# DLRM tower with a compressed interaction network: the first MLP layer in high and low halves, and the third cross layer's halves divided anew

## What is computed

```python
x0 = e                                   # (512, 39, 16)
for W in (f0, f1, f2):                   # (39*39,128), (128*39,128), (128*39,128)
    z = einsum('bfd,bgd->bfgd', x0, xk).reshape(b, f * g, d)
    xk = einsum('bpd,pm->bmd', z, W); outs.append(xk)
z = sum(concatenate(outs, axis=1), axis=-1)            # (512, 384)
h = concatenate([z, dense_ctx], axis=1)                # (512, 400)
h = maximum(h @ W_top1 + b_top1, 0)                    # 512 wide
h = maximum(h @ W_top2 + b_top2, 0)                    # 256 wide
y = h @ W_top3
```

## Time and profile before

| | us |
|---|---|
| median of 3 runs | 659.19 |
| lowest, highest | 656.44, 663.04 |
| the profiled execution | 662.05 |
| its span, first to last instruction | 660.1 |

### The profile page before, as it was taken

One profiled execution on the slowest core, in us unless ns is written; L12 is line 12 of the kernel. 1 busy time (PEld: TensorE's weight loads), 2 busy tenths in 40 slices (PEclk: granted clock), 3 DMA queues, 4 the chain that ended last, 5 costly groups with the idle time before them and its releaser, 6 DMA issues.

```text
span 660.1 us, 12277 instructions
## 1 busy us (share of the span) xinstructions
PE 629.3 (95%) x2653; PEld 488.4 (74%) x2653; DVE 541.1 (82%) x1224; ACT 541.4 (82%) x1884; POOL 480.6 (73%) x453
## 2 busy tenths in 40 slices
PE   0879899999999999999999999999999999999898
PEld 0467588888888888888888888888888888773673
DVE  0669779898898989898989898989889898996870
ACT  1457679989898989898989898989989898994762
POOL 5888879898988989898989898989878652002330
PEclk9989999999999999999999999999999999996999
DMA  8336522313122232313132213231313303002000
GB/s 217 66 72 128 118 75 44 81 42 81 42 62 61 53 70 45 78 21 89 23 81 42 75 42 81 42 81 42 81 41 68 102 1 97 18 0 77 1 0 1
DMA packets 65502, 40.32 MB, mean 61 GB/s; under 512 B 37486, under 2 KB 50480, under 8 KB 65482
## 3 DMA queue, kind: packets, MB, share of 16 engines
q1 hardware_dynamic: 54201, 35.37, 22.2%
q0 software_dynamic: 5184, 1.29, 2.1%
q10 hardware_dynamic: 6097, 3.44, 2.1%
HBM read 38.13 MB, written 1.94 MB: 61 GB/s over the span
## 4 chain that ended last, share of the span: by engine, by line
PE 89%; DMA 3%; DVE 2%; issue 2%; SPq 1%; ACT 1%; POOL 1%; ACTq 0%; DVEq 0%
PE psa L916 13%; PE psa L912 13%; PE psa L913 13%; PE psd L912 8%; PE psd L916 8%; PE psd L913 8%; PE psg L886 5%; PE ps L850 4%; PE ps L849 4%; PE ps L851 3%; PE psg L976 1%; DMA x_rows_first<-emb_tiles 1%; PE psg L970 1%; PE psg L971 1%; PE psd L991 1%
## 5 line engine op out<-in xcount | busy, mean ns | idle before, releaser
L730 ACT ACTIVATE parts<-psa,x0c 128x128 f32<-128x128 f32 x1536 | 449.1, 457 | 56.4 <-PE psa L916 51.8
L606 DVE SCALAR_TENSOR_TENSOR parts<-psd,x0c,parts 128x128 f32<-128x128 f32 x960 | 265.9, 342 | 54.3 <-PE psd L916 52.4
L577 DVE TENSOR_REDUCE cur<-parts 128x64 f32<-128x1536 f32 x128 | 223.6, 1747 | 6.5 <-DVE parts L606 2.5
L912 PE MATMUL psa<-w1h,x1h 128*128 128x512 f32 x384 | 168.9, 440 | 2.0 <-ACT parts L730 1.5
L413 POOL TENSOR_TENSOR z0l<-pairs,z0h 117x512 fp32r<-117x512 f32 (+1 forms) x98 | 126.8, 1303 | 42.7 <-ACT z0h L683 42.0
L916 PE MATMUL psa<-w1h,x1l 128*128 128x512 f32 x384 | 152.4, 397 | 3.2 <-DVE x1l L567 3.2
L913 PE MATMUL psa<-w1l,x1h 128*128 128x512 f32 x384 | 151.4, 394 | 0.0
L394 POOL DMA_INDIRECT emb<-tables,idx x130 | 126.4, 972 | 24.3 <-issue 24.3
L403 POOL TENSOR_TENSOR pairs<-x0t,pairs 117x512 f32<-117x512 f32 (+1 forms) x98 | 126.7, 1302 | 3.0 <-DMA x0t<-x_rows 2.2
L912 PE MATMUL psd<-w1h,x1h 128*128 128x512 f32 (+1 forms) x256 | 100.9, 394 | 0.6 <-DVE parts L606 0.6
L916 PE MATMUL psd<-w1h,x1l 128*128 128x512 f32 (+1 forms) x256 | 97.6, 381 | 0.0
(11 more groups left out here) (91 smaller groups left out, 574.3 us busy)
## 6 DMA issues: line engine op xcount, KB each, us to landing
pairs<-x_rows SPq DMA_DIRECT2D x105, 156.0 KB
pairs<-x_rows SPq DMA_DIRECT2D x30, 234.0 KB
x0t<-x_rows SPq DMA_DIRECT2D x45, 78.0 KB
gram<-w ACTq DMA_DIRECT2D x3, 832.0 KB, 7.7
emb<-tables,idx POOLq DMA_INDIRECT x130
pairs<-x_rows_first SPq DMA_DIRECT2D x8, 136.5 KB
x_rows<-emb SPq DMA_DIRECT2D x13, 72.0 KB, 2.2
wt_sb<-w_top SPq DMA_DIRECT2D x1, 768.0 KB, 6.1
```

Of the source, the lines that this page charges most:

```text
L577: return dve.tensor_reduce(cur1[:, t % 2, first:end], terms[:, first:end, :, :], AX.XY, ALU.add)
L606: op = dve.scalar_tensor_tensor(acc, y[:, M * j:M * j + M], x0c[:, t, GF * g + j:GF * g + j + 1], acc, ALU.mult, ALU.add)
L730: op = act.activation(lanes(dst, j), y[:, M * j:M * j + M], ACT.Copy, scale=x0c[:, t, GF * g + j:GF * g + j + 1])
L912: pe.matmul(y[:, 0:n], hi, w1h[:, c], start=True, stop=False)
```

## The change

- The first MLP layer is computed in halves. ScalarE makes the high halves of its weights in the last block: parts 0, 3, 1 and 2 at the places `TOP_HIGH_AT` (tile, number of the a-group) and the high halves of s0 and of the dense features at `TOP_IN_HIGH_AT`. GpSimd makes the low halves, between its `spread`s of the last block.
- Dense features and bias are one matmul: 17 rows (16 features and a row of ones; the weights have the bias as row 17) are stored three times, at partitions 0, 32 and 64, as high, low, high of the features against high, high, low of the weights. The bias load and the bias operand of the Relu go.
- Ahead of the third layer stand 16 float32r matmuls instead of 8 plain ones, with the last gram ahead of the fourth part instead of the third; behind it stand 12 for layer 2's sums (high half by ScalarE and low half by GpSimd, at row 19) and 12 for s2 (high half by ScalarE, low half by VectorE).
- w2 is divided in ten chunks of four rows, in a ring of four. A string gives each chunk's high half ("a" ScalarE, "d" VectorE, "p" GpSimd: two, five, three of them) and another its low half (seven on VectorE, three on GpSimd). GpSimd takes twelve rows' low halves instead of nine. The ring of rows has five slots.

```diff
+DENSE_ROWS, DENSE_END = 17, 81
+TOP_HIGH_AT = {(0, 2): 0, (0, 4): 3, (1, 2): 1, (1, 4): 2}
+TOP_IN_HIGH_AT = {(2, 2): 0, (2, 4): 1}
...
-W2_CHUNK, W2_RING = 7, 3
+W2_CHUNK, W2_RING = 4, 4
 W2_CHUNKS = [(f, min(f + W2_CHUNK, F)) for f in range(0, F, W2_CHUNK)]
-W2_AHEAD = 3
-L2_RING = 4
+W2_HIGH_BY, W2_LOW_BY = "dpadapddpd", "ddddpdpdpd"
+W2_EARLY_CHUNKS = 3
+W2_HIGH_AHEAD, W2_LOW_AHEAD = 6, 5
+ROWS_ON_POOL = (0, 2, 5, 7, 11, 15, 18, 23, 29, 31, 35, 37)
+L2_RING = 5
...
-    return f % 4 == 3
+    return f in ROWS_ON_POOL
...
-        dense_sb = x0t[0:16, :]
-        s2 = parts[:, 0, 3 + H2T, :]
+        dense_sb = x0t[0:DENSE_END, :]
+        dense_h = w0h[0:DENSE_END, 0:B]
+        s0h, s0l = w0l[:, 0:B], z0l[:, 3 * H1T * 128:3 * H1T * 128 + B]
+        s1h, s1l = x1h[:, :], x1l[:, :]
...
+        def top_high(part, m):
+            at = H1T * 128 * part + 128 * m
+            return z0h[:, at:at + 128] if part < 3 else z0h[0:DENSE_END, at:at + 128]
+        def top_low(part, m):
+            at = H1T * 128 * part + 128 * m
+            return z0l[:, at:at + 128]
...
-            sp.dma_start(wt1_sb[0:16, 3, :], wt1[384:400, :]).then_inc(mlp_in, 16)
+            sp.dma_start(wt1_sb[0:DENSE_END, 3, :], wt1d).then_inc(mlp_in, 16)
...
-            sp.dma_start(dense_sb, dense).then_inc(mlp_in, 16)
+            sp.dma_start(dense_sb, dense).then_inc(dense_in, 16)
...
+            def top_low_part(part):
+                pool.wait_ge(wt1h_ready, [1, 3, 4][part])
+                n = H1T * 128
+                c = slice(n * part, n * part + n)
+                pool.tensor_tensor(z0l[:, c], wt1_sb[:, part, :], z0h[:, c].bitcast(F32), ALU.subtract).then_inc(wt1l_ready, 1)
+            def mixed_top_low_part():
+                pool.wait_ge(wt1h_ready, 2)
+                mixed = z0h[64:DENSE_END, 3 * H1T * 128:4 * H1T * 128]
+                pool.tensor_tensor(mixed, wt1_sb[64:DENSE_END, 3, :], mixed.bitcast(F32), ALU.subtract).then_inc(wt1l_ready, 1)
             pool.memset(x0c[:, :, F:FX], 1.0).then_inc(ones_ready, 1)
             pool.wait_ge(ids_in, 16)
             pool.tensor_tensor(idx_tiles[:, :], tile_ids, tile_base, ALU.add).then_inc(idx_ready, 1)
                 gather_early(0, c)
             pool.wait_ge(ones_ready, 1)
-            pool.wait_ge(const_in, 16 * 4)
+            pool.wait_ge(const_in, 16 * 3)
             first_block()
             with pool.Fori(1, NBLK - 3) as b:
                 block_of(b, True, True, True, bass.ds((b + 2) * CH, CH))
             block_of(NBLK - 3, True, True, False)
             block_of(NBLK - 2, True, False, False)
-            block_of(NBLK - 1, False, False, False)
-            pool.wait_ge(w2h_ready, 1)
-            pool.tensor_tensor(w2_slot(w1l, 0), w2_part(*W2_CHUNKS[0]), w2_slot(w1h, 0).bitcast(F32),
-                               ALU.subtract).then_inc(w2l_pool, 1)
+            spread(NBLK - 1, 0)
+            top_low_part(0)
+            pool.wait_ge(wt1l_ready, 1)
+            mixed_top_low_part()
+            pool.wait_ge(wt1l_ready, 2)
+            spread(NBLK - 1, 1)
+            top_low_part(1)
+            top_low_part(2)
+            spread(NBLK - 1, 2)
+            pool.wait_ge(top_in_high, 1)
+            pool.tensor_tensor(s0l, s0[:, :], s0h.bitcast(F32), ALU.subtract).then_inc(top_in_low, 1)
+            pool.wait_ge(top_in_high, 2)
+            pool.wait_ge(top_in_low, 1)
+            low = w0h[32:64, 0:B]
+            pool.tensor_tensor(low, x0t[32:64, :], low.bitcast(F32), ALU.subtract).then_inc(top_in_low, 1)
+            pool.wait_ge(top_in_low, 2)
+            def w2_high(i):
+                if i >= W2_RING:
+                    pool.wait_ge(l2_steps, W2_CHUNKS[i - W2_RING][1])
+                if W2_CHUNKS[i][1] > W2_EARLY:
+                    pool.wait_ge(w2b_in, 16)
+                pool.tensor_copy(w2_slot(w1h, i), w2_part(*W2_CHUNKS[i])).then_inc(w2h_ready["p"], 1)
+            def w2_low(i):
+                pool.wait_ge(w2h_ready[W2_HIGH_BY[i]], w2_turn(i, W2_HIGH_BY))
+                pool.tensor_tensor(w2_slot(w1l, i), w2_part(*W2_CHUNKS[i]), w2_slot(w1h, i).bitcast(F32),
+                                   ALU.subtract).then_inc(w2l_ready["p"], 1)
+            pool.wait_ge(w2a_in, 16)
+            pool.wait_ge(y_a, NBLK * NA - SLOTS + 2)
+            pool.wait_ge(y_d, NBLK * ND - D_OFF[TILES] + D_OFF[TILES - 1] + 1)
+            for i in range(W2_EARLY_CHUNKS):
+                if W2_HIGH_BY[i] == "p":
+                    w2_high(i)
+                if W2_LOW_BY[i] == "p":
+                    w2_low(i)
+            spread(NBLK - 1, 3)
             for f in range(F):
+                for i in range(W2_EARLY_CHUNKS, len(W2_CHUNKS)):
+                    if W2_HIGH_BY[i] == "p" and f == max(W2_CHUNKS[i][0] - W2_HIGH_AHEAD, 0):
+                        w2_high(i)
+                    if W2_LOW_BY[i] == "p" and f == max(W2_CHUNKS[i][0] - W2_LOW_AHEAD, 0):
+                        w2_low(i)
                 if on_pool(f):
                     pool.wait_ge(gh_ready, f + 1)
                     if f >= L2_RING:
                         pool.wait_ge(l2_steps, f - L2_RING + 1)
                     pool.tensor_tensor(gram_slot(w1l, f), gram[:, f, :], gram_slot(w1h, f).bitcast(F32),
                                        ALU.subtract).then_inc(gl_pool, 1)
+                if f == F // 2:
+                    pool.wait_ge(s1h_ready, 1)
+                    pool.tensor_tensor(s1l, gram[:, F, :], s1h.bitcast(F32), ALU.subtract).then_inc(s1l_ready, 1)
...
-                for i in range(1, len(W2_CHUNKS)):
-                    if f == (W2_CHUNKS[i - 1][0] - W2_AHEAD if i > 1 else 0):
-                        dve.wait_ge(w2h_ready, i + 1)
+                for i in range(len(W2_CHUNKS)):
+                    if W2_HIGH_BY[i] == "d" and f == max(W2_CHUNKS[i][0] - W2_HIGH_AHEAD, 0):
                         if i >= W2_RING:
                             dve.wait_ge(l2_steps, W2_CHUNKS[i - W2_RING][1])
+                        dve.wait_ge(w2a_in, 16)
+                        dve.wait_ge(w2b_in, 16)
+                        dve.tensor_copy(w2_slot(w1h, i), w2_part(*W2_CHUNKS[i])).then_inc(w2h_ready["d"], 1)
+                    if W2_LOW_BY[i] == "d" and f == max(W2_CHUNKS[i][0] - W2_LOW_AHEAD, 0):
+                        dve.wait_ge(w2h_ready[W2_HIGH_BY[i]], w2_turn(i, W2_HIGH_BY))
                         dve.tensor_tensor(w2_slot(w1l, i), w2_part(*W2_CHUNKS[i]), w2_slot(w1h, i).bitcast(F32),
-                                          ALU.subtract).then_inc(w2l_dve, 1)
+                                          ALU.subtract).then_inc(w2l_ready["d"], 1)
...
+            dve.wait_ge(s2h_ready, 1)
+            dve.tensor_tensor(gram_slot(w1l, 0), psg[:, :], gram_slot(w1h, 0).bitcast(F32), ALU.subtract).then_inc(s2l_ready, 1)
...
+            def top_high_part(part):
+                act.wait_ge(mlp_in, 16 * 2)
+                act.wait_ge(l0_steps, L0T * NBLK)
+                n, rows = H1T * 128, 128 if part < 3 else DENSE_END
+                act.activation(z0h[0:rows, n * part:n * part + n], wt1_sb[0:rows, part, :], ACT.Copy).then_inc(wt1h_ready, 1)
+            def top_in_high_part(i):
+                if i == 0:
+                    act.wait_ge(s0_summed, NBLK)
+                    act.activation(s0h, s0[:, :], ACT.Copy).then_inc(top_in_high, 1)
+                else:
+                    act.wait_ge(dense_in, 16)
+                    act.activation(dense_h, dense_sb, ACT.Copy).then_inc(top_in_high, 1)
...
+                        if ends(b) and (t, n) in TOP_HIGH_AT:
+                            top_high_part(TOP_HIGH_AT[t, n])
+                        if ends(b) and (t, n) in TOP_IN_HIGH_AT:
+                            top_in_high_part(TOP_IN_HIGH_AT[t, n])
...
-            act.dma_start(bt1_sb[:, :], bt1).then_inc(const_in, 16)
...
-            w2_high(0)
+            for i in range(W2_RING):
+                if W2_HIGH_BY[i] == "a" and W2_CHUNKS[i][0] <= W2_HIGH_AHEAD + 2:
+                    w2_high(i)
             for T in range(NBLK * TILES - 2, NBLK * TILES):
                 gram_out(T, slice(T * TB, (T + 1) * TB))
-                if T == NBLK * TILES - 2:
-                    w2_high(1)
             act.wait_ge(g2_copied, NBLK * TILES)
             for f in range(F):
-                for i in range(2, len(W2_CHUNKS)):
-                    if f == W2_CHUNKS[i - 1][0] - W2_AHEAD:
+                for i in range(len(W2_CHUNKS)):
+                    if W2_HIGH_BY[i] == "a" and f + W2_HIGH_AHEAD == W2_CHUNKS[i][0] > W2_HIGH_AHEAD + 2:
                         w2_high(i)
                 if f >= L2_RING:
                     act.wait_ge(l2_steps, f - L2_RING + 1)
                 act.activation(gram_slot(w1h, f), gram[:, f, :], ACT.Copy).then_inc(gh_ready, 1)
+                if f == F // 2:
+                    act.activation(s1h, gram[:, F, :], ACT.Copy).then_inc(s1h_ready, 1)
             act.wait_ge(l2_steps, F)
```

(91 more changed lines are left out.)

## The result

The changed kernel takes 662.2 us (median of 20 runs, 659.3 to 667.1), the kernel before 659.0 (20 runs): a ratio of 1.0048, interval 1.0031 to 1.0065. So it is slower by about 3.2 us, where 659.5, that is +0.3, was forecast. The time lies within the 1% that was called likeliest, near the upper end of the range of that forecast (655.5 to 663).

The account below looks back on a forecast made before the run. Third layer bound by the summed subtraction and copy time of VectorE and GpSimd, which exclude each other: layer end +1.7, behind it -1.4, so +0.3 on the median 659.19, giving 659.5 us; own range 655.5 to 663, 8 in 10 650 to 666.5.

Parts of the forecast that it names:

- What bounds the low halves: Third layer: VectorE and GpSimd subtractions with both inputs in SBUF exclude each other; the pair is occupied 97%.
- the 1.09 + 0.60 of the prediction: Third layer: one subtraction costs the pair of engines 1.09 us on GpSimd, 0.60 on VectorE.
- One sign: Third layer: TensorE's waits total over 10 us, with low halves as releasers.
- Part 1: Last block: ScalarE's six copies delay the last sum about 1.4 us, to 601.1; ends 0 and 2.1.
- Part 2: First MLP matmuls in halves: third layer can start at 602.8, 5.9 us earlier than before.
- Part 3: Third layer after 602.8: pair time 39.7 us, with idle time and last matmul 41.2, ending at 644.0.
- Part 4: Behind the third layer: 24 matmuls at 0.23 (5.5 us) for 8 at 0.86 (6.9), so -1.4.
- the pair's sum: Third layer: summed time of VectorE's and GpSimd's subtractions and copies, 39.7 us.
- A: Third layer: pair doesn't bind, layer runs at TensorE's pace to 631.7; time about 647; chance 0.2 including up to 652.6.
- B: Third layer and behind: starved TensorE, clock halved; 665.5, or 667 with one more stretch; chance beyond 665.8 is 0.15.
- C: Before the last gram: clock falls, gram and four matmuls take twice as long, +1.4, 661; within the forecast's 0.65.

Follow-up runs that it names:

- run 4: Changed kernel with all low halves of the third layer's rows and weights on VectorE, weights' high halves on ScalarE: 651.4 us, ratio 0.9883 to the kernel before.
- run 5: Changed kernel with 20 rows' low halves on GpSimd instead of 12: 659.8 us, ratio 1.0073 to the kernel before.
- run 6: Kernel before with the nine rows' low halves moved from GpSimd to VectorE: 656.1 us, ratio 0.9955.
- run 7: On top of run 4, ScalarE's six high halves for the first MLP layer in the last block made by GpSimd: 649.5 us, ratio 0.9869 to the kernel before.
- run 1: Kernel before, unchanged, for a second trace of its end: 660.9 us.
- the other two traces with plain matmuls: Changed kernel with first MLP layer in plain float32 (661.0 us, ratio 1.0031), and run 6.
- run 9: On top of run 4, a ring of three rows instead of five: one execution, 646.1 us, where the kernel before took 654.9.

## Why the prediction was right, and where a step was off

**What bounds the low halves: right.** VectorE and GpSimd at the start of the layer in the changed kernel, as in the earlier trace rows:

```profile
607.49 1.76 DVE L765 TENSOR_TENSOR w1l<-gram,w1h 128x512 fp32r<-128x512 f32 x1
609.18 1.77 DVE L765 TENSOR_TENSOR w1l<-gram,w1h 128x512 fp32r<-128x512 f32 x1
610.87 0.41 DVE L756 CAST w1h<-pairs 128x512 fp32r<-128x512 f32 x1
...
626.97 1.50 DVE L756 CAST w1h<-parts 128x512 fp32r<-128x512 f32 x1
```

```profile
606.98 1.72 POOL L629 TENSOR_TENSOR w1l<-gram,w1h 128x512 fp32r<-128x512 f32 x1
608.67 1.73 POOL L629 TENSOR_TENSOR w1l<-gram,w1h 128x512 fp32r<-128x512 f32 x1
...
628.14 0.80 POOL L602 CAST w1h<-parts 128x512 fp32r<-128x512 f32 x1
```

GpSimd's ends lie at 608.70 and 610.40, VectorE's at 609.25 and 610.95: each waits for the other's end, so a pair takes 1.70, the 1.09 + 0.60 of the prediction. By the two timelines one of the engines is busy at every moment of the layer up to the end of its last low half (642.94), as forecast; the sum had allowed 1.2 us of idle time, which were not there. Runs 4, 5 and 6 move the layer in both directions (29.4, 40.2 and 43.6 us for 0, 12 and 20 rows), and so the mechanism is shown, not argued. One sign missed its number: TensorE's waits were to be over 10 us in all, and its matmul records show 8.4 for low halves. The Trainium skill's rule ("SBUF — State Buffer", section "Who interferes with whom") is what the trace has here.

**Part 1, the lag: right, a little large.** VectorE's sums of the first tiles of the block with their waits for ScalarE, and two of ScalarE's copies:

```profile
567.61 1.75 DVE L668 TENSOR_REDUCE cur<-parts 128x64 f32<-128x1536 f32 x1
...
575.55 1.75 DVE L668 TENSOR_REDUCE cur<-parts 128x64 f32<-128x1536 f32 x1 [0.44 <-ACT parts L843]
...
583.47 1.75 DVE L668 TENSOR_REDUCE cur<-parts 128x64 f32<-128x1536 f32 x1 [0.61 <-ACT parts L843]
...
591.15 1.75 DVE L668 TENSOR_REDUCE cur<-parts 128x64 f32<-128x1536 f32 x1 [0.38 <-ACT parts L843]
```

```profile
579.13 0.69 ACT L803 ACTIVATE z0h<-wt_sb 128x512 fp32r<-128x512 f32 x1
...
581.65 0.75 ACT L803 ACTIVATE z0h<-wt_sb 128x512 fp32r<-128x512 f32 x1
```

Three waits of 0.44, 0.61 and 0.38 instead of none; with what VectorE regains, 30.93 - 29.78 = 1.2 us, against 1.4. Run 7 takes them away. The last sum ended at 601.96 instead of 601.1 because block 15's first sum came 1.0 us later in this execution (567.61 for 566.60), which the change has no part in as far as is known.

**Part 2, the start: the sum right, the gain wrong.** From the last sum's end (598.54 + 3.42 = 601.96) to the layer are 2.1 us, where 1.7 were predicted. The gain was counted from 608.70 of the one profiled execution: 5.9. Against run 1, the interval goes from 4.9 to 2.1, by 2.7, and the lag takes 1.2 of that: 1.5 gained. **This is the term that was mis-sized**, by 4.4 us. The prediction put the profiled execution 2.9 above the median and took these for a constant that both kernels share; they lay in the very stretch that was being compared, as 13.6 us of half clock, of which run 1 has 3.4 and the other two traces with plain matmuls none. With the 1.5 in its place and all else as predicted the sum would have come to 663.9, just outside the 655.5 to 663 of this forecast; that the measured 662.2 lies inside is in part luck.

**Part 3, the layer: right.** 41.2 predicted from its start, 40.2 measured. VectorE's copies take 0.41, with 0.33 to the next start, where VectorE finds the way free, against the 0.4 taken; behind GpSimd's they take 1.50, which the pair's sum holds already. GpSimd's of weights take 0.80 and 1.07.

**Part 4, behind the layer: right.** 649.83 - 644.29 = 5.5 for 24 matmuls, where 5.5 was predicted and 6.9 stood before.

**The sum again, against run 1.** Lag +1.2, start -2.7, layer 40.2 - 32.8 = +7.4, behind it -1.3: +4.6, of which 3.2 were measured (interval 2.0 to 4.3). The 1.4 left over are not explained; both sides are one execution each, and those of the kernel before lie between 655.8 and 663.0.

**The rivals.** A (side by side) falls with runs 4 to 6. B had the clock falling in the layer: in the changed kernel it stayed at 1.00 with TensorE busy 31.57 of 40.19, so it didn't decide, but with 20 rows it happened (0.92). C didn't occur: the clock was 1.00 from 61 us to the end. What makes the clock fall at the end with plain matmuls in one execution for 13.6 us, in another for 3.4 and in two not at all was not settled.

## What to carry to other kernels

Before work goes from VectorE to GpSimd, look at both timelines for instructions that end just behind each other's end: there the two are one resource, and GpSimd's dearer instruction makes it slower (here a row cost 1.09 instead of 0.60, and with all low halves back on VectorE and the weights' high halves on ScalarE the layer shrank from 40.2 to 29.4 us, 2.1 of which the high halves alone had given). GpSimd's idle time is good for copies and subtractions where VectorE has at most one input in SBUF (run 7). And before the terms of a sum are taken from one profiled execution, compare its time and mean clock with the others', or take a second trace: if it is an outlier (one that lies apart from the rest), the excess has a place, and it may be just where the change is.

## What the runs showed of the hardware beyond that

In run 4 GpSimd's one subtraction of 128 x 512 took 16.20 us, from 615.81 to 632.01. VectorE's last row ended at 630.86, so GpSimd's ran only behind that one; until then VectorE's instructions followed one another with no gap in the records. In run 7, on another chip, it took 16.21. In run 9, with a ring of three rows, it took 1.78. In the changed kernel GpSimd never waited longer than one instruction of VectorE. So GpSimd can be kept out for as long as VectorE has instructions lined up, but isn't always.

Theory S, that GpSimd gets its turn only where VectorE pauses, forecast the 1.78, but the records don't bear out its reason. In the rows of the changed kernel shown above VectorE's next instruction has its start at 609.18, before the end of the one ahead of it at 609.25, just as in run 4, and yet GpSimd's of 608.67 goes first. In run 9, too, VectorE shows no gap at GpSimd's turn: its instruction ahead ends at 611.95, its next one starts at 611.86, and the last gap before that is 0.05 us at 610.0. What decides the turn is therefore open; a pause too short for the records isn't ruled out, and no run changed the gaps and nothing else. A single instruction left on GpSimd beside a full VectorE can be late by the length of VectorE's queue: in run 4 the layer's last matmul started at 631.57, and the next, which could have followed 0.23 later, waited until 632.07 for it.
